# Two-layer attention kernel: the order of value products, projection pieces, MLP units, row copies and channel sums between the turns

## The reference, cut to what matters

```python
x = x + attention0(group_norm(x))      # layer 0
x = x + deformable(group_norm(x))      # layer 1

# layer 0: 8 heads of 64, 1024 tokens
qkv = xs @ Wqkv + bqkv
attn = softmax(q @ k.T / 8)            # 1024 x 1024 per head
out = (attn @ v) @ Wout + bout

# layer 1, in 16 windows of 8 x 8 pixels, 8 groups:
q = wq @ layer_norm(x)
off = 4 * tanh(pw @ gelu(depthwise_conv(q) + b))     # 4 sampled points per group
kv = grid_sample(x, grid + off); k = wk @ kv; v = wv @ kv
pos = sign(d) * log1p(|d|)                           # d: pixel minus point, two numbers
bias = w3 @ relu(w2 @ relu(w1 @ pos + b1) + b2) + b3 # the MLP, 128 wide
out = w_out @ (softmax(q.T k / 8 + bias) v) + b_out
```

## Time and profile before

| | |
|---|---|
| median of 3 runs | 3783.43 us (3781.56 to 3785.04) |
| profiled execution, its own time | 3796.79 us |
| its span | 3795.0 us |
| TensorE busy | 3378.8 us, 89% |
| VectorE, ScalarE, GpSimd busy | 60%, 43%, 6% |
| TensorE's granted clock, mean share | 0.968 |
| moved by DMA | 192.19 MB, mean 51 GB/s |

### The profile page before, as it was taken

How to read it: one execution, slowest core, us unless ns; L and a number is a source line. 1 busy time by engine, 2 the same in 40 slices (tenths; PEclk the granted TensorE clock), 3 DMA queues, 4 the chain that set the end, 5 groups by cost and what they waited for, 6 DMA issues and landing times.

```text
span 3795.0 us, 50087 instructions
## 1 busy us (share of the span) xinstructions
PE 3378.8 (89%) x20128; PEld 2159.9 (57%) x20128; DVE 2273.7 (60%) x2965; ACT 1640.5 (43%) x2338; POOL 221.6 (6%) x165
## 2 busy tenths in 40 slices
PE   4998798899988999889998899988999899997978
PEld 3665566555665556645665556654566555663544
DVE  4664667466565565566665756647566475664664
ACT  1552544263443545343542535426344263442533
POOL 0000020001000020000200002000020000200200
PEclk9999999999999999999999999999999999997979
DMA  4112012301123011220112211121112301103020
GB/s 160 26 48 61 20 30 65 95 23 32 30 65 94 23 36 34 92 59 34 34 48 80 48 45 30 48 92 29 46 30 70 96 13 42 30 11 94 12 63 34
DMA packets 141239, 192.19 MB, mean 51 GB/s; under 512 B 80177, under 2 KB 100148, under 8 KB 139444
## 3 DMA queue, kind: packets, MB, share of 16 engines
q1 hardware_dynamic: 141012, 188.99, 17.4%
HBM read 145.62 MB, written 43.32 MB: 50 GB/s over the span
## 4 chain that ended last, share of the span: by engine, by line
PE 75%; DVE 9%; DMA 7%; ACT 4%; issue 3%; SPq 1%; POOL 0%; ACTq 0%; DVEq 0%; POOLq 0%
PE banks L549 12%; PE banks L599 12%; PE banks L614 11%; PE banks L583 10%; PE banks L558 8%; PE banks L766 4%; DMA x_dram<-exps 3%; PE banks L776 3%; PE banks L767 3%; PE banks L768 3%; PE banks L647 2%; DMA recips_dram<-recips 2%; PE banks L755 2%; PE banks L745 1%; PE banks L814 1%
## 5 line engine op out<-in xcount | busy, mean ns | idle before, releaser
L1234 DVE TENSOR_REDUCE neg_max<-banks 128x1 f32<-128x1024 f32 x512 | 602.4, 1218 | 250.3 <-PE banks L583 243.1
L958 ACT ACTIVATE exps<-banks,neg_max 128x1024 f32<-128x1024 f32 x512 | 564.9, 1112 | 211.8 <-DVE neg_max L1234 211.7
L599 PE MATMUL banks<-ident,exps 128*128 128x128 f32 x4096 | 566.3, 282 | 69.3 <-DVE exps_turned L1243 49.2
L599 PEld LDWEIGHTS banks<-ident,exps 128*128 128x128 f32 x4096 | 449.7, 143 | 246.0 <-issue 244.3
L968 ACT ACTIVATE exps_turned<-banks 128x1024 f32<-128x1024 f32 x256 | 262.0, 1024 | 756.6 <-PE banks L599 755.9
L614 PE MATMUL banks<-exps_turned,values 128*64 128x256 f32 x4096 | 511.2, 394 | 15.1 <-DVE exps_turned L1243 8.3
L583 PE MATMUL banks<-qk_halves 64*128 64x512 f32 x3072 | 437.6, 417 | 93.3 <-ACT exps L958 49.0
L1243 DVE COPY exps_turned<-banks 128x1024 f32<-128x1024 f32 x256 | 312.8, 1222 | 226.8 <-PE banks L599 226.0
L583 PEld LDWEIGHTS banks<-qk_halves 64*128 64x128 f32 x3072 | 287.3, 189 | 216.9 <-issue 178.1
L1400 DVE SCALAR_TENSOR_TENSOR qk_halves<-banks,qk_halves 128x1024 fp32r<-128x1024 f32 x256 | 312.1, 1222 | 151.3 <-ACT qk_halves L1005 150.3
L614 PEld LDWEIGHTS banks<-exps_turned,values 128*64 128x64 f32 x4096 | 282.3, 140 | 174.4 <-issue 68.6
(11 more groups left out here) (163 smaller groups left out, 3627.9 us busy)
## 6 DMA issues: line engine op xcount, KB each, us to landing
wqk_ring<-wqk_split SPq DMA_DIRECT2D x64, 512.0 KB, 4.4
x_image<-in_x SPq DMA_DIRECT2D x8, 2048.0 KB, 9.1
recips_b<-recips_dram SPq DMA_DIRECT2D x256, 64.0 KB, 3.8
exps_turned<-in_x SPq DMA_DIRECT2D x32, 512.0 KB, 7.8
x_dram<-exps SPq DMA_DIRECT2D x32, 512.0 KB, 2.6
exps_turned<-x_dram SPq DMA_DIRECT2D x32, 512.0 KB, 20.0
out<-exps_turned SPq DMA_DIRECT2D x32, 512.0 KB, 2.6
wv_halves<-wv_split SPq DMA_DIRECT2D x6, 2048.0 KB, 9.8
```

The lines of the kernel that those rows point to most:

```text
L599: mm = pe.transpose(TB[:, kt // 4, kt % 4 * P:kt % 4 * P + P], PB[:, 2 * h + n % 2, kt * P:(kt + 1) * P], IDENT[:])
L958: freed(act.activation(PB[:, 2 * h + n % 2], slot(("s", m, i)), ACT.Exp, bias=NM[:, m:m + 1], accum_out=SS[:, m:m + 1]), ("s", m, i))
L1234: dve.tensor_reduce(NM[:, m:m + 1], slot(("s", m, i)), AX.X, ALU.max, negate=True).then_inc(mx, 1)
```

## The change

The work is the same but for its order. In the list of TensorE, in even steps from 2 on a whole value product (32 matmuls of the profile) stands between the turns, and in odd steps to 21 a whole piece (12 matmuls); nothing but small products follows turn 1. The first piece of an image stands whole ahead of step 0; its high and low halves follow the first exps and maxima. The six row copies are spread over steps 6 to 11, and their way to DRAM goes behind the reciprocals u = 6. The statistics are taken 4, 2 and 2 at a time in steps 24 to 26 (before 2, 4, 2); the group sum is made at the end of step 26 into free columns of `OB`, the variance in step 27 ahead of the copy, and the first two normalisings at its end. The rows of the MLP are loaded in two parts (columns for two rounds, and the rest) by 24 DMAs, and the residual's loads wait for both. The MLP makes the first layer of two units (a round) at once, with the halves of its results in four places of `QK` instead of two, and `mlp3` moves in between the last two second-layer halves.

```diff
 def piece_of(n):
     p, j = n // KT + 1, n % KT
-    return (p, j // 2, j % 2) if p < PAIRS else None
+    return (p, j // 2) if p < PAIRS and j % 2 == 0 else None
...
+        def h1_hi_half(u):
+            return QK[:, u // 2 % 2, u % 2]
+
+        def h1_lo_half(u):
+            return QK[:, u // 2 % 2, 2 + u % 2]
...
             def load_rows(j):
                 sp.wait_ge(rows_out, (j + 1) * 16 * PTS)
-                for s in range(4):
-                    for d in range(3):
-                        sp.dma_start(RR[32 * s + ROWS * d:32 * s + ROWS * d + ROWS], rows_dram[:, s]).then_inc(rows_in, 16)
+                for part, cols in enumerate((slice(0, FIRST_ROWS), slice(FIRST_ROWS, WIN * C))):
+                    for s in range(4):
+                        for d in range(3):
+                            sp.dma_start(RR[32 * s + ROWS * d:32 * s + ROWS * d + ROWS, cols], rows_dram[:, s, cols])\
+                                .then_inc(rows_in[part], 16)
...
-                    if u == 4 and i:
+                    if u == 6 and i:
                         rows_to_dram(i - 1)
...
                 if i:
+                    rows_landed(sp, i)
                     load_residual(i - 1)
...
-                mm = project_halves(MB, w, c, (2 * half, 2 * half + 1))
-                if half == 1:
-                    mm.then_inc(piece_full, 1)
+                project_halves(MB, w, c, range(CT)).then_inc(piece_full, 1)
...
-                if f == 0 and j + 2 < B:
-                    pe.wait_ge(gn_var, 2 * j + 4)
...
-                pe.wait_ge(rows_in, (j + 1) * 192)
+                pe.wait_ge(rows_in[0], (j + 1) * 192)
                 mlp1(0)
+                mlp2(0, 0)
+                mlp2(0, 1)
                 mlp1(1)
-                for u in range(UNITS):
-                    mlp2(u)
-                    if u + 2 < UNITS:
-                        mlp1(u + 2)
-                    if u % 2 and u >= 3:
-                        mlp3(u // 2 - 1)
+                mlp2(1, 0)
+                mlp2(1, 1)
+                for v in range(1, WIN):
+                    if v + 1 < WIN:
+                        mlp1(v + 1)
+                    mlp2(2 * v, 0)
+                    mlp2(2 * v, 1)
+                    mlp2(2 * v + 1, 0)
+                    mlp3(v - 1)
+                    mlp2(2 * v + 1, 1)
                 mlp3(WIN - 1)
...
                     turn(n, 0, i)
-                    if n >= 2:
-                        value_product(n // 2 - 1, n % 2, i)
+                    if n >= 2 and n % 2 == 0:
+                        for half in range(2):
+                            value_product(n // 2 - 1, half, i)
+                    if piece_of(n + 1):
+                        piece(n + 1, i)
...
-                    if i + 1 < B and n == 27:
-                        wait_after(pe, kz_done, i)
-                        group_sums(2 * i + 2)
...
                     turn(n, 1, i)
-                    if piece_of(n + 1):
-                        piece(n + 1, i)
...
+                    if i + 1 < B and n == 26:
+                        group_sums(2 * i + 2, GSO)
...
-                    if i and n == 6:
-                        log_rows(i - 1)
+                    if i and 6 <= n < 12:
+                        log_row((n - 6) // 2, (n - 6) % 2, i - 1)
```

More of the change, by code:

```diff
@@ L31 @@
 MAXES = 12
+FIRST_ROWS = 2 * C
 SBUF_END = 228096
@@ L944, in high_piece @@
             def high_piece(n, i):
-                p, which, _ = piece_of(n)
+                p, which = piece_of(n)
                 c, first = 512 * (which % 2), 4 * (which // 2)
@@ L1602, in _ @@
             log_split(B - 1)
-            log_rows(B - 1)
+            for part in range(3):
+                for o in range(2):
+                    log_row(part, o, B - 1)
             weights_turned(B - 1)
```

134 lines of the change are left out of this document (72 added, 62 removed).

## The result

The changed kernel took 3660.25 us (median of 4 runs, 3658.74 to 3666.05) against 3782.49 us of the kernel before (median of 4, 3779.56 to 3785.04): a ratio of 0.968, 95% interval 0.9663 to 0.9697, 122 us less. The forecast was 3631 with a range of 3600 to 3705: the direction is right and the time lies in the range, but 29 us above the number and 5 us outside the forecast's own range of 3605 to 3655.

The account below looks back on a forecast made before the run. TensorE, busy 89%, was taken as the bound, with time lost in its waits and between blocks. Terms 26 + 40 + 18 + 36 + 28 + 16 - 12 = 152 off the profiled 3796.8, less 13.4, gave about 3631 us; range 3600 to 3705.

Parts of the forecast that it names:

- Whole blocks and boundary: Middle steps and pair boundaries: whole products and pieces win 26 us; removing 24 waits for q and k wins 40.
- rival 4: Middle steps: turn 1's copy misses its 2.61 us by 0.3, costing 67 us, 3698 in all; chance 0.07.
- rival 1: Outputs of each pair: reciprocals come late, 1.0 us more per pair, 84 us, 3715 in all; chance 0.12.
- rival 2: Reciprocals' round trips: each overlaps the next, 269 us lost, kernel slower at 3900; chance 0.04.
- The term of 18: Steps 6 to 11: spreading the six row copies wins 3.1 less 0.5 us in 7 images, 18 us.
- First piece: Image start: the whole first piece ahead of scores costs 1.2 us; with 0.3 for table loads, 12 lost in all.
- Late steps: Steps 24 on: 62.0 to 56.4 us in middle images, image 0 gains, image 7 loses 3.5; 36 won.
- the 6 us for image 0: Image 0's late steps: 50.8 us instead of 57.1, counted as 6 within the late steps' 36.
- Start of the MLP: MLP's first relu: split row loads and a later residual bring it 4.0 us earlier in 7 images, 28 us.
- Rival 5: MLP row loads: short loads cost as much as long ones, 112 us lost, 3743 in all; chance 0.04.
- rival 3: MLP: wins nothing, as the store lands late and VectorE holds the body; 28 + 16 lost, 3675; chance 0.14.
- MLP body: MLP rounds: two units in 4.50 us instead of 4.81, partly taken back by VectorE; 16 us won.

Follow-up runs that it names:

- e2: Changed kernel with all six row copies back in step 6: 3708.29 us, ratio 0.9815 of the kernel before.
- e1: Kernel before with only the whole value products in even steps and whole pieces in odd steps: 3766.25 us, ratio 0.9972.
- e7: Changed kernel with each image's first piece behind turn 0 of step 0: 3633.32 us, ratio 0.9614 of the kernel before.
- e12: Kernel before with matmuls nobody reads around the MLP's start (8, 20 and 8 per image): 3764.92 us, ratio 0.9962.
- e6: Changed kernel with half value products in steps 24, 25 and 28 to 31: 3654.85 us, ratio 0.968 of the kernel before.
- e10: Changed kernel with first piece in step 0, 20 unread matmuls per image and half value products in steps 28 and 29: 3617.76 us, 0.9577 of before.
- e11: e10 with the MLP one unit at a time, as before the change: 3622.56 us, ratio 0.9587 of the kernel before.
- e8: Changed kernel with 20 unread matmuls per image around the MLP's start, keeping TensorE busy: 3635.46 us, ratio 0.9628 of the kernel before.
- e3: Changed kernel with the MLP's rows in 12 long loads and the residual loaded at once: 3668.87 us, ratio 0.9707 of before.
- e4: Changed kernel with the MLP one unit at a time, rows still in two parts: 3654.71 us, ratio 0.9671 of before.
- e5: Changed kernel run again, unchanged, on another chip: 3650.28 us, ratio 0.9669 of the kernel before.

## Why the forecast was right, and where it was off

**Whole blocks and boundary.** The two lengths of step (7.23 and 6.26) were right to 0.02, from the block lengths of the earlier trace rows; the middle value for the piece (2.8) was right too (2.84). The 24 waits went. The copy of turn 1 fits (rival 4), and the round trip was in time: the outputs follow 13.4 us behind their reciprocal in the middle steps, as the pair is long, and the trip of 22 us in image 4 was a single event, neither in every pair (rival 1) nor carried on from pair to pair (rival 2). Long waits for the reciprocals at the end of images 1 and 2 (11.2 and 8.8) are not of the change: before had 10.3 and 8.2 there.

**Row copies: the right total by the wrong share.** The term of 18 priced the old order by its wait of 3.10 alone, and I took 0.5 us an image for what stays; nothing stays, and the old order lost more than the wait. The step with it took 10.05 instead of 6.90, and the next one 8.45 in most images (6.91 to 9.68), without any idle time but at a granted clock of 0.80, as this window of before shows (the clock is the third number from the end):

```profile
...
1410.99:1419.44 8.45, 8.45 (x51) 6.11 (x52) 3.72 (x4) 3.21 (x5) 6.09 (x5) 0.80 0.00 0
...
```

That is 4.8 an image, 34 in all, so the term was too small by some 16. What balanced it in the row of steps 0 to 23 were the dearer first piece, the table loads and a low clock at the start of an image (37 us at 1.2 GHz in the first four steps of after's images, 20 in before's): luck, not the working. And e2 shows that in the new order they would cost 51 to 55, and e1 that the whole blocks alone win 10, not 54. The terms are no separate gifts. Each of the short steps has less slack on VectorE, and the moves of copies and statistics are what lets the blocks pay. My walk through the steps took the new order as a whole and so came near the sum, with the luck just told; whoever had made the blocks alone by my terms would have been wrong by 44. From one end the parts are 10 (blocks alone), 52 (row copies), about 34 (statistics, 5.7 in each of 6 images by the steps of e1 and of after; no run moves the statistics alone, so this part is read from two traces and not shown), 10 to 14 (rows and store) and about 5 (pairs), together 111 to 115 of 122 to 125. As the first is added to the old kernel and the others are taken from the new one, that they add up so nearly proves nothing by itself.

The Trainium skill (SBUF — State Buffer, Who interferes with whom) has VectorE's copies blocked for the length of one GpSimd instruction each. The trace agrees, for the single copies too. GpSimd's pixel instructions last 1.3 each. The first and the third copy began inside one and ended 0.14 and 0.16 behind it, so they took 0.69 and 1.29; the second fell between two and took 0.41; the last three, behind the work, took 0.41, 0.28 and 0.41. In a row (e2) the first took 0.69 and each of the next five 1.34 to 1.50: the next GpSimd instruction had begun 0.11 to 0.25 before each of them. So the spread copies are cheaper inside GpSimd's work (3.5 instead of 7.5 for the six) because each meets at most the rest of one instruction, and the 0.69 and 0.41 of the first two, for which I took 1.4 each, are where they happened to fall.

**First piece.** Priced at 1.2, measured 1.36 an image (11.40 for 10.04). What I overlooked is that it needn't be lost: e7 puts it into the waits of step 0 and wins 17. The table loads around the log make step 5 7.50 long: 1.26 over an odd step of 6.24, where before it was 0.60 over 6.90, so 0.7 more and not 0.3.

**Late steps.** Forecast 56.4, 50.8 and 44.0; measured 56.11 in the cleanest of the images in the middle (mean 56.9), 50.50 and 43.89. The lengths are right, the loss in image 7 too. But the 6 us for image 0 were not won by the change. The 57.09 of before hold the wait of 8.57 for a late trip; e12, which has the old order, takes 49.81 in the same window:

```profile
...
260.28:310.09 49.81, 42.31 (x335) 30.06 (x335) 39.87 (x56) 27.35 (x40) 1.01 (x1) 1.00 0.11 21
...
```

So I priced a single event of the profiled execution as a gain, and probably twice, since it also lies in the 13.4 by which that execution was over its median; that would be 6 of the 29 us (no trace of another execution of before shows it). The whole products are not what sets the late steps: e6 and e10 take them apart and win nothing.

**Start of the MLP.** The first relu comes 24.7 earlier over 7 images, forecast 28; the rest is the x2 store, which still lands late in three images. Rival 5 (short loads cost as much as long) and rival 3 are out. The Trainium skill (SBUF — State Buffer, The DMA setup-cost knee) would have had the first rows 24 us behind the first issue (an estimate from its 2 us of fixed cost) if the short loads paid one after another; the first layer starts 19.0 behind it and waits for the pixels' copy, not for rows, so they were not paid one after another.

**MLP body: the term that was too large.** 4.48 for two units was forecast as 4.50. But in place of 16 the profiles show 9, and e11 against e10 about 5. The step that failed is what the start and the end take back: with the rounds at 0.33 less from third layer to third layer, the time from the first relu to the first third-layer block rose from 12.4 to 13.4 and the last two blocks take 2.2 more, since a second-layer block and its relu now stand between them. I had counted 2.5 for VectorE and nothing for the ends; in the 13 blocks between, VectorE took back next to nothing (58.7 us instead of 62.9, 0.32 a block of the 0.33).

**What had no term: a low clock and single events.** 6.3 us were lost between values and pixels' copy (a late trip in image 1 and turns at 1.2 GHz), 8.7 in one late trip, which the late trip of before in image 0 offsets. As a whole the clock was no loss of the change: 244 us at 1.2 GHz in before's profile, 210 in after's, and e12 wins 10 in the kernel before with a filler like that with which e8 wins 15 in the changed one, so at most about 5 of the shortfall is a clock that the new order meets more often. It meets it more often in one place, the pixels' turns: they ran slow in one of the images 1 to 6 in before and in four in after. The idle time ahead of them is the same 2.2 us in both, so why it costs the clock in one image and not in the next stays open.

## What to carry to other kernels

When a step is made shorter, price every side job anew by the slack of the short step: a job that cost 4.8 us in the old order cost 8.3 in the new one. Price it by the length of the steps and not only by the wait, and look for a single event of the profiled execution in the stretch that a term is taken from. A list of terms can have the right sum while no term is what its part is worth alone; take one part away from the finished kernel and put one alone into the old kernel before saying which one won. And where a piece of work is to be placed, look for a wait next to it: the first piece, moved 3 us back into two waits, won 17 us on top of the 122 of the whole change.

## What the runs showed of the hardware

Ahead of the pixels' turns of images 1 to 6 TensorE stood idle for 2.2 us, at a granted clock of 1.00 in nearly all of them, and then often went on at 1.2 instead of 2.4 GHz: the same 32 turns took 5.4 to 5.8 instead of 4.43, and later 128x512 matmuls at the low clock followed each other by 0.43 instead of 0.23. The turns were slow in one of the six images in before and e1, in three in e3 and e6, in four in after, e4 and e5, in five in e2 and e7, and in none of the six in e8 to e12, where matmuls without use had cut the idle time to 0.43. Twenty such matmuls per image around the start of the MLP won 15 us (0.4%) in the changed kernel and a similar filler 10 us (0.3%) in the kernel before.

The same 64x512 copy on VectorE took 0.28 to 0.41 without GpSimd. One that began while a GpSimd instruction ran ended 0.14 to 0.28 us behind that instruction: 0.32 to 1.30 singly, by where it fell (after, e5 and e7), and 1.34 to 1.50 for each of five behind one another (e1 and e2), as each met a fresh instruction of 1.3 us.
